# Twelve mixing groups by split f32r products, and a reordered last attention group and end, in a fused attention and soft-MoE kernel

## The reference

```python
q, k, v = mlp_q(x), mlp_k(x), mlp_v(x)            # each: gelu(x @ W1 + b1) @ W2 + b2
scores = einsum('bid,bjd->bij', q, k) / sqrt(256 * 512)
scores = scores * tril(ones)                       # mask by product, no softmax
a = layernorm(einsum('bij,bjd->bid', scores, v)) * ln_w + ln_b
x1 = layernorm(x + a)
xn = layernorm(x1) * gamma + beta                  # MoE, 16 experts x 16 slots
logits = einsum(unit(xn) * scale, unit(mu))        # 2048 x 256 per batch
dispatch, combine = softmax(logits, tokens), softmax(logits, slots)
slot_in = einsum('bnd,bnes->besd', xn, dispatch)
slot_out = gelu(slot_in @ w1 + b1) @ w2 + b2
out = layernorm(x1 + einsum('besd,bnes->bnd', slot_out, combine))
```

## Time and profile before

| | us |
|---|---|
| median of 3 runs | 590.18 |
| profiled execution | 590.34 |
| its span, first to last instruction | 588.6 |
| TensorE busy | 572.5 (97%) |
| VectorE busy | 485.6 (83%) |
| ScalarE busy | 393.4 (67%) |
| GpSimd busy | 393.9 (67%) |
| mean granted clock of TensorE | 0.996 |

### The profile page before, as it was taken

One profiled execution on the slowest core, in us unless ns is written; L12 is line 12 of the kernel. 1 busy time (PEld: TensorE's weight loads), 2 busy tenths in 40 slices (PEclk: granted clock), 3 DMA queues, 4 the chain that ended last, 5 costly groups with the idle time before them and its releaser, 6 DMA issues. The chain is left out here.

```text
span 588.6 us, 11698 instructions
## 1 busy us (share of the span) xinstructions
PE 572.5 (97%) x3796; PEld 528.0 (90%) x3796; DVE 485.6 (83%) x1048; ACT 393.4 (67%) x855; POOL 393.9 (67%) x395
## 2 busy tenths in 40 slices
PE   9999999999999999999999999979999999999994
PEld 7889989999999999999998999968999999888883
DVE  6579889899898898888989989979988777557885
ACT  4765666676766667667677666567688777435765
POOL 0869779789797797787977978785646443104453
PEclk9999999999999999999999999999999999999998
DMA  8324134043141331422403403105555555923445
GB/s 234 81 73 108 22 87 99 12 107 43 65 107 18 89 71 41 102 33 74 107 13 94 86 23 74 26 11 98 84 72 72 73 73 73 147 33 108 143 144 179
DMA packets 163473, 47.04 MB, mean 80 GB/s; under 512 B 139470, under 2 KB 159340, under 8 KB 163436
## 3 DMA queue, kind: packets, MB, share of 16 engines
q1 hardware_dynamic: 163424, 46.57, 36.9%
q10 hardware_dynamic: 12, 0.00, 0.0%
HBM read 21.39 MB, written 8.39 MB: 51 GB/s over the span
## 5 line engine op out<-in xcount | busy, mean ns | idle before, releaser
L523 POOL TENSOR_TENSOR h_lo<-xn_all,h_hi 128x512 fp32r<-128x512 f32 x32 | 41.4, 1295 | 68.2 <-ACT xn_all L649 67.1
L647 ACT ACTIVATE h_hi<-bank,bias_col 128x512 fp32r<-128x512 f32 x96 | 66.4, 692 | 18.8 <-PE bank L793 17.1
L791 PE MATMUL bank<-xnT_hi,w_hi 128*128 128x512 f32 x188 | 76.2, 405 | 0.0
L792 PE MATMUL bank<-xnT_lo,w_hi 128*128 128x512 f32 x188 | 74.4, 396 | 0.0
L793 PE MATMUL bank<-xnT_hi,w_lo 128*128 128x512 f32 x188 | 74.2, 395 | 0.0
L682 ACT CAST state_hi<-bank 128x512 fp32r<-128x512 f32 x57 | 33.5, 588 | 50.1 <-PE bank L926 50.1
L1608 PE MATMUL bank<-xn_all,e_tok 128*128 128x257 f32 x256 | 65.1, 379 | 0.0
L1190 DVE TENSOR_TENSOR state_lo<-bank,state_hi 128x512 fp32r<-128x512 f32 x57 | 39.4, 691 | 29.0 <-ACT state_hi L682 29.0
L1686 PE MATMUL bank<-w_sb,ET_all 128*128 128x256 f32 x256 | 55.4, 379 | 0.0
L1686 PEld LDWEIGHTS bank<-w_sb,ET_all 128*128 128x128 f32 x256 | 48.6, 190 | 6.6
L1507 ACT ACTIVATE e_tok<-bank,shift,xinv 128x256 f32<-128x256 f32 x64 | 36.1, 565 | 27.3 <-PE bank L1598 20.5
(11 more groups left out here) (202 smaller groups left out, 2081.6 us busy)
## 6 DMA issues: line engine op xcount, KB each, us to landing
x_all<-in_L_attn_x SPq DMA_DIRECT2D x16, 512.0 KB, 3.9
kT<-k_turn SPq DMA_DIRECT2D x128, 64.0 KB, 2.5
ET_all<-e_turn SPq DMA_DIRECT2D x64, 128.0 KB, 3.8
xn_all<-in_xT SPq DMA_DIRECT2D x15, 512.0 KB, 4.7
out<-xn_all SPq DMA_DIRECT2D x15, 512.0 KB, 3.0
w_sb<-in_L_ffn_w SPq DMA_DIRECT2D x2, 512.0 KB, 5.3
...
```

What stands on the lines that cost most here:

```text
L523: pool.tensor_tensor(h_lo[:, V_SLOT, m, :], hv[:, m, :], h_hi[:, V_SLOT, m, :].bitcast(F32), ALU.subtract).then_inc(hv_split, 1)
L647: nc.scalar.activation(h_hi[:, h_slot(j, n), m, :], ps, ACT.Gelu, bias=bias(n, m))
L791: nc.tensor.matmul(ps, w[0], xs[0], start=start, stop=False, skip_group_check=shared)
L792: nc.tensor.matmul(ps, w[0], xs[1], start=False, stop=False, skip_group_check=shared)
```

## The change

In batches 1 to 3 (groups 4 to 15) the mixing product is made of three f32r products, from parts of the combine weights (`ET_hi` by ScalarE's `round_e`, `ET_lo` by GpSimd's `split_e`) and of the slots' outputs (`so_hi` by ScalarE's copy, `so_lo` by VectorE). `ET_hi` takes the place of `x1_all` and `ET_lo` that of `ET_all`; so x1 of these groups is written to DRAM by SP (`spill_x1`, in the routing) and read back into other places (`reload_x1`, ahead of and in the mixing). In the last attention group the division of group 1's tokens goes from GpSimd to ScalarE, half a bias sum goes to the routing, and the orders on GpSimd, ScalarE and VectorE are changed. At the end one sum of the last group moves ahead of a wait, the four normalisations of the last group are shared out otherwise, and ScalarE's queue stores its first pair. The diff, cut to its core:

```diff
+with nc.sbuf_tensor("ET_hi", [P, GROUPS, SB * GT, P], F32R) as place:
+    ET_hi = place
...
 def add_beta(engine, k, q):
-    engine.wait_ge(tok_scaled, GT * k + GT)
+    if k == 1:
+        engine.wait_ge(tok_weighted, 1)
+    else:
+        engine.wait_ge(tok_scaled, GT if k == 0 else GT * k)
...
-        def divide_tokens(k, q):
-            pool.wait_ge(x1_ready, GT * k + 3 * GT)
-            pool.wait_ge(r2_ready, k + 3)
-            pool.wait_ge(hv_split, 2 * GROUPS)
-            pool.tensor_tensor(xn[q][:, :, 0:D], x1_all[:, GT * k:GT * k + GT, :],
-                               r2_all[:, GT * k:GT * k + GT].unsqueeze(2).to_broadcast([P, GT, D]),
-                               ALU.mult).then_inc(tok_divided, 1)
...
             pool.tensor_tensor(xn[q][:, :, 0:D], xn[q][:, :, 0:D],
                                g_rows[:, :].unsqueeze(1).to_broadcast([P, GT, D]), ALU.mult
-                               ).then_inc(tok_scaled, GT)
+                               ).then_inc(tok_weighted, 1)
         def body(g, j, ba, attend=True, project=True, settle=True, more=True):
             a = g - 1
             if not project:
+                add_beta(pool, 1, 1)
                 split_vsum(a, 1)
-                add_beta(pool, 1, 1)
+                invert_norms(pool, 0, 0, minus_half[:, :])
                 return
             if attend:
                 split_vsum(a, 0)
...
             if attend:
-                add_ln_b(g)
+                add_ln_b(g, range(2) if more else range(1))
             if not more:
-                divide_tokens(1, 1)
                 weight_tokens(1)
             split_ktok(g, 0)
+            if attend:
+                invert_o(pool, a, 1)
             if not more:
                 split_v(g, 0)
-            if attend:
-                invert_o(pool, a, 1)
             split_ktok(g, 1)
...
+        def divide_tokens(k, q, tiles):
+            act.wait_ge(x1_ready, GT * k + 3 * GT)
+            act.wait_ge(r2_ready, k + 3)
+            act.wait_ge(hv_split, 2 * GROUPS)
+            for t in tiles:
+                tile = GT * k + t
+                nc.scalar.activation(xn[q][:, t, 0:D], x1_all[:, tile, :], ACT.Copy,
+                                     scale=r2_all[:, tile:tile + 1]).then_inc(tok_divided, 1)
...
-                apply_z(act, a - 2, ja % 2, (0,))
                 round_state(ba, i + 2, tail_hi[2])
                 round_masked(a)
                 round_vsum(a, 1)
-                apply_z(act, a - 2, ja % 2, (1, 2))
+                apply_z(act, a - 2, ja % 2, (0, 1))
                 round_state(ba, i + 3, tail_hi[3])
-                apply_z(act, a - 2, ja % 2, (3,))
+                apply_z(act, a - 2, ja % 2, (2, 3))
...
                 if not more:
-                    norms(act, 0, 0, range(GT))
+                    norms(act, 0, 0, (0, 1))
+                    divide_tokens(1, 1, range(GT))
                 follow(3)
             round_ktok(g)
+            if not more:
+                norms(act, 0, 0, (2, 3))
             round_v(g, 0)
...
                     sum_v(g, j, 0)
+                    sum_v(g, j, 1)
+                    return
                 add_out(dve, a, 2)
                 add_out(dve, a, 3)
-                if not more:
-                    return
                 z_summed(dve, a, 1)
...
             tail_state(1)
             mask_scores(a)
-            sum_v(a, ja, 1)
             sum_v(a, ja, 2)
             tail_state(2)
             split_masked(a)
+            add_out(dve, a - 1, 2)
+            add_out(dve, a - 1, 3)
+            tail_state(3)
             split_xnT(dve, 0, 0)
-            tail_state(3)
+            floor_norms(dve, 0, 0)
             dve.wait_ge(v_split, 2 * GROUPS)
             scale_tokens(2, 2)
...
+    FIRST = GB * SPLIT[0]
+    SPLIT_GROUPS = range(FIRST, GB * SPLIT[-1] + GB)
+    AGAIN = 2 * GB
+    x1_spill = nc.dram_tensor("x1_spill", [len(SPLIT_GROUPS), P, GT, D], F32, kind="Internal").ap()
+    x1_again = [e_turn[0][:, :, :, :, :].rearrange("p f s t c -> p (f s t c)"),
+                e_turn[1][:, :, :, :, :].rearrange("p f s t c -> p (f s t c)"),
+                x1_over_xnT[:, 0, :, :].rearrange("p t d -> p (t d)"),
...
+        def spill_x1(g):
+            sp.wait_ge(tok_scaled, GT * g)
+            n = g - FIRST
+            if n > 1:
+                sp.wait_ge(x1_spilled[n % 2], 16 * (n // 2))
+            sp.dma_start(x1_spill[n], x1_all[:, GT * g:GT * g + GT, :]).then_inc(x1_spilled[n % 2], 16)
+        def reload_x1(g):
+            n = g - FIRST
+            if g < AGAIN:
+                sp.wait_ge(logits_done, TILES)
+                for i in range(2):
+                    sp.wait_ge(e_moved[i], 16 * FOUR * GROUPS // 2)
+                    sp.wait_ge(x1_spilled[i], 16 * (n // 2 + 1))
+            else:
+                sp.wait_ge(mixed, GT * (g - AGAIN) + GT)
+                sp.wait_ge(x1_spilled[n % 2], 16 * (n // 2 + 1))
+            if n > 1:
+                sp.wait_ge(x1_reloaded[n % 2], 16 * (n // 2))
+            sp.dma_start(x1_again[g], x1_spill[n]).then_inc(x1_reloaded[n % 2], 16)
...
         for g in range(GROUPS):
+            if g + GB - 1 in SPLIT_GROUPS:
+                spill_x1(g + GB - 1)
...
                                  w2.rearrange("(r two) h d -> two h r d", two=2)[w]).then_inc(w2_loaded, 16)
+        for g in range(FIRST, AGAIN):
+            reload_x1(g)
         for k in range(LAST):
+            if k + AGAIN in SPLIT_GROUPS:
+                reload_x1(k + AGAIN)
             sp.wait_ge(y_normed, GT * k + GT)
             sp.dma_start(out_t[:, GT * k:GT * k + GT, :], y[k % GB][:, :, 0:D]).then_inc(stored[k % GB], 16)
-        for pair in range(2):
-            at = GT * LAST + 2 * pair
-            sp.wait_ge((y_normed, last_normed)[pair], (GT * LAST + 2, 2)[pair])
-            sp.dma_start(out_t[:, at:at + 2, :], y[LAST % GB][:, 2 * pair:2 * pair + 2, 0:D]
-                         ).then_inc(stored[LAST % GB], 16)
+        sp.wait_ge(last_normed, 3)
+        sp.dma_start(out_t[:, GT * LAST + 2:GT * LAST + 4, :], y[LAST % GB][:, 2:4, 0:D]
+                     ).then_inc(stored[LAST % GB], 16)
         for q in range(GB):
             sp.wait_ge(stored[q], 16 * B + (16 if q == LAST % GB else 0))
...
             pool.memset(xn[q][:, :, D:D + 1], 1.0).then_inc(ones_set, 1)
+        def split_e(g):
+            pool.wait_ge(e_rounded, g - FIRST + 1)
+            exact = ET_all[:, g, :, :]
+            pool.tensor_tensor(ET_lo[:, g, :, :], exact, ET_hi[:, g, :, :].bitcast(F32), ALU.subtract
+                               ).then_inc(e_split, 1)
...
                     add_beta(pool, GB * b + q + 3, (q + 3) % GB)
+                if GB * b + q - 2 in SPLIT_GROUPS and not (last and q == GB - 1):
+                    split_e(GB * b + q - 2)
+                if b == 0 and q == 0:
+                    xp = x1_all[:, GT * (GROUPS - 1) + 2:GT * GROUPS, :]
+                    pool.tensor_tensor(xp, xp, lnb_rows[:, :].unsqueeze(1).to_broadcast([P, 2, D]),
+                                       ALU.add).then_inc(xb_ready, 1)
                 if b == 0 and q == 2:
                     invert_z(pool, GROUPS - 2, 0)
...
             pool.memset(hs_blank[w], 0.0).then_inc(hs_blanked, 1)
+        pool.wait_ge(hs_blanked, 2)
+        for g in range(GROUPS - GB + 1, GROUPS):
+            split_e(g)
         def add_residual(k):
...
             yk = y[k % GB][:, SUMMED, 0:D]
-            pool.tensor_tensor(yk, yk, x1_all[:, GT * k + SUMMED, :], ALU.add).then_inc(y_added, 1)
+            x1 = x1_all[:, GT * k + SUMMED, :]
+            if k in SPLIT_GROUPS:
+                pool.wait_ge(x1_reloaded[(k - FIRST) % 2], 16 * ((k - FIRST) // 2 + 1))
+                x1 = x1_again[k][:, SUMMED, :]
+            pool.tensor_tensor(yk, yk, x1, ALU.add).then_inc(y_added, 1)
         def invert_deviation(k):
...
                     norms(act, k, q, (2, 3))
+            if t % GT == GT - 1 and k - 3 in SPLIT_GROUPS and not (last and q == 0):
+                round_e(k - 3)
+        def round_e(g):
+            n = g - FIRST
+            act.wait_ge(e_moved[g % 2], 16 * FOUR * (g // 2 + 1))
+            act.wait_ge(x1_spilled[n % 2], 16 * (n // 2 + 1))
+            nc.scalar.copy(ET_hi[:, g, :, :], ET_all[:, g, :, :]).then_inc(e_rounded, 1)
         def route(b, last):
...
         route(B - 1, last=True)
+        round_e(GROUPS - GB + 1)
+        round_e(GROUPS - GB + 2)
         for half in range(2):
             act.wait_ge(hs_biased, 2 * half + 2)
             act.wait_ge(hs_blanked, 2)
             pairs = slice(half * PAIRS // 2, (half + 1) * PAIRS // 2)
             nc.scalar.activation(hs[:, pairs, :], hs[:, pairs, :], ACT.Gelu).then_inc(hs_ready, 1)
+        round_e(GROUPS - 1)
         for n in range(4):
             act.wait_ge(so_done, n + 1)
-            nc.scalar.copy(so[:, n, :, :], so_ps[n][:, :].rearrange("p (s d) -> p s d", s=SB)
```

(57 more changed lines are left out.)

32 lines of the change are left out of this document (27 added, 5 removed).

## The result

| | before | after |
|---|---|---|
| median of the runs, us | 590.36 (4 runs) | 583.24 (582.8 to 584.8, 4 runs) |
| ratio, with 95% interval | | 0.9884 (0.9872 to 0.9896) |
| profiled execution, us | 590.34, span 588.6 | 584.80, span 582.7 |

The account below looks back on a forecast made before the run. TensorE was taken to bound routing and mixing, with gaps at the end of attention. Attention -2.0, mixing -7.0, Gelu +0.6 and end +0.15 sum to -8.25: 581.9 us for the median, range 581.0 to 588.5.

Parts of the forecast that it names:

- TensorE in the mixing: Groups 4 to 15: three f32r products replace each float32 product, 2.866 us a group instead of 3.455; booked -7.0 us.
- Routing: Spills, rounding casts and subtractions for the mixing's parts fit into waits and free stretches of the routing; cost 0.
- Rivals 2 and 3: Casts, subtractions or spills delay routing's exponentials, 583 to 586 us, chance 0.13; spills delay the exchange, 591 and above, 0.04.
- Attention: Last attention group: division on ScalarE and new orders start the routing's first matmul about 2.0 us earlier; booked -2.0 us.
- First Gelu: Between routing and mixing: casts of groups 13 and 14 ahead of the first Gelu delay it; booked +0.6 us.
- The end: After the last matmul: last normalisation ends about 4.15 us later, today 3.95; booked +0.15 us (-0.3 to +0.4).
- DMA: Spills in the routing and reloads ahead of and in the mixing hold nothing up; both booked at 0.
- the midway case: Mixing: a run falls into rival 1 midway, 584 to 587 us; a third of that rival's 0.25.
- rival 1: Mixing: nm_y waits for GpSimd's residual, 3.42 us a group; twelve groups give 0.4 instead of 7.0; 588.4 us; chance 0.25.

Follow-up runs that it names:

- the forced order: The changed kernel, with GpSimd's residual of each mixing group made to wait for nm_y of the group before: 585.18 us, ratio 0.9916.
- the order lost: The changed kernel, with VectorE's nm_y made to wait for GpSimd's residual of the following mixing group: 590.97 us, ratio 1.0008.

## Why the prediction was right or wrong

The time fell within the range and by the mechanism that was forecast, f32r products 0.119 apart in the mixing and an earlier end of attention; the size of two terms was off. I take the second profiled execution of the changed kernel (span 580.8, not tipped) against that of before (588.6).

- **TensorE in the mixing: right, a little low.** The price taken from attention, 0.1194, was 0.1183 to 0.119. From group 3's deviation to the last matmul's end before is 580.9 - 541.5 = 39.4 us, after it 571.80 + 0.28 - 540.04 = 32.0: 7.35 saved, where 7.0 was booked.
- **Routing: right.** From its first matmul to the last reciprocals of its columns are 115.84 us before and 115.85 after. Twelve spills (the forecast said nine), nine casts and nine subtractions cost nothing, with the DMA share at 0.74 instead of 0.58 (397 to 514 us). Rivals 2 and 3 did not occur.
- **Attention: right in kind, high by 0.3.** 1.7 was saved from the `square` row to the routing (21.39 to 19.66) in every profile. The first profile of the changed kernel shows where 0.3 went, as its `square` row stands where that of before does (376.77). Weighting started earlier than forecast (379.38, not 379.66: the division took 1.71 us, not 2.06). Yet the first update came at 385.44 instead of 385.1, since `ve_o`, to which the forecast gave no time, took 1.02 us and held back the bias sum of the values. The wait for `split_vsum`, which the forecast had until 392.3, lasted until 393.08, as `add_beta` ended at 391.69 and not before 391. TensorE's last matmul ended at 395.93 instead of 395.0, and so TensorE, not VectorE's scaling (395.57, forecast 395.5), closed the stage. With both put right 1.4 us more are gained.
- **First Gelu: right.** +0.6 forecast; the casts last 1.99 for two and the Gelu came 0.49 late. Moving the casts gave all of it back.
- **The end: wrong, by 0.9.** Forecast: 4.15 us from the last matmul to the last normalisation's end, where there were 3.95, and nothing for the store: +0.15. Measured: 576.75 - 572.08 = 4.67, and the span ends 4.05 behind that instead of 3.75: +1.0. Where group 14's deviation would stand was right: 0.40 us ahead of the last matmul's end (571.68 against 572.08). What failed is the list behind it: three sums of 0.48, not two of 0.42, and the small operations between the large ones, which the forecast left out.
- **The sum of the rows.** The `square` row stands 0.24 us earlier in this execution than in that of before, and the change didn't do that: the changed kernel's first profile has it at 376.77. -0.24 - 1.73 (attention) + 0.49 (Gelu) - 7.35 (mixing) + 1.02 (end) = -7.8, the difference of the spans.
- **DMA: wrong at 0.** The reloads fill the engines for 20 us and stores land in 4.1 us instead of 2.9. In the changed kernel this had a price only through the 0.06 us between `nm_y` and the residual: 1.65 us where that order tips. The forecast gave the midway case a place in rival 1 but looked for its trigger in summed delays of hundredths, not in a store.
- **Outside the span.** What an execution takes beyond its span was 1.7 to 1.8 us before and 2.0 to 2.2 with the changed kernel, in every run. It explains 0.3 us of the shortfall. I didn't find its cause: it is 1.8 to 2.0 with the end undone, back at 1.7 to 1.8 in the kernel with the forced order, and 2.35 to 2.44 with the order lost.

Together: +0.9 (end), +0.3 (attention), -0.35 (mixing) and -0.1 (Gelu) are 0.7, of which the early start of this execution's last attention group, luck, hides 0.24: its span is 7.8 shorter and not 8.25. The 0.3 outside the span brings the shortfall to 0.75. The medians are another 0.4 to 0.7 above this execution's 582.83, which fits that luck and the tipped executions; how it divides between them the runs don't settle. That the forecast missed by no more than this is luck in part: the mixing gave 0.35 more than was booked, against the end's 0.9.
